# Layer 0's causal mask of natural scores as 32 constant rows of their stacks, and values in frames of 27 columns that fill one output bank

## The reference

```python
scores = jnp.einsum('bhqd,bhkd->bhqk', q, k) / jnp.sqrt(jnp.float32(D))
causal = jnp.tril(jnp.ones((T, T), dtype=bool))
scores = jnp.where(causal, scores, -jnp.inf)
weights = jax.nn.softmax(scores, axis=-1)
out = jnp.einsum('bhqk,bhkd->bhqd', weights, v)
out = out.transpose(0, 2, 1, 3).reshape(B, T, C)
return out @ Wo + bo
```

## Time and profile before

| | |
|---|---|
| median of 3 runs | 495.09 us (494.87 to 496.61) |
| the profiled execution | 494.89 us, of which its span is 493.2 us |
| mean granted TensorE clock | 0.985 |
| TensorE matmul busy | 435.5 us (88%), 3261 instructions |
| VectorE busy | 316.4 us (64%) |
| ScalarE busy | 240.3 us (49%) |
| GpSimd busy | 188.2 us (38%) |
| chain that ended last, by engine | PE 67%, VectorE 12%, DMA 8%, issue 5%, ScalarE 4% |

### The profile page before, as it was taken

The page is one execution under the profiler, slowest core; times in us unless marked ns, Lnnn a source line. Parts: engine busy times, 40 slices in busy tenths (PEclk is TensorE's granted clock), DMA queues, the critical chain, the costliest instruction groups (busy, mean ns, idle before and its releaser), DMA issues.

```text
span 493.2 us, 9895 instructions
## 1 busy us (share of the span) xinstructions
PE 435.5 (88%) x3261; PEld 304.1 (62%) x3261; DVE 316.4 (64%) x955; ACT 240.3 (49%) x565; POOL 188.2 (38%) x234
## 2 busy tenths in 40 slices
PE   1578799997989999999999997999988999999985
PEld 1454446764566576665666655556548999998642
DVE  4555770117577687786877788767565776765753
ACT  2511355444556556554555444445453555555552
POOL 6570120002143543644545451656431444545000
PEclk9999999999899999999999999999998999999987
DMA  5444452325273763623256452142242122211341
GB/s 173 144 97 133 127 134 65 113 77 143 65 183 105 155 180 112 160 85 95 84 158 170 156 152 89 43 128 86 61 122 67 54 77 55 77 50 33 90 131 51
DMA packets 55216, 52.76 MB, mean 107 GB/s; under 512 B 5312, under 2 KB 50000, under 8 KB 55168
## 3 DMA queue, kind: packets, MB, share of 16 engines
q1 hardware_dynamic: 44208, 35.12, 25.7%
q10 hardware_dynamic: 8528, 12.03, 8.6%
q0 software_dynamic: 2432, 5.01, 3.3%
HBM read 33.09 MB, written 19.04 MB: 106 GB/s over the span
## 4 chain that ended last, share of the span: by engine, by line
PE 67%; DVE 12%; DMA 8%; issue 5%; ACT 4%; SPq 2%; POOL 1%; ACTq 0%; DVEq 0%
PE ps_P L1616 8%; PE ps_N L1747 6%; PE ps_N L1549 5%; PE ps_M L1788 3%; DVE NM L1155 3%; PE ps_P L1757 3%; PE ps_M L1757 3%; PE ps_N L1555 3%; PE ps_S L1580 3%; PE ps_N L1560 3%; PE ps_S L1594 3%; PE ps_S L1747 3%; PE ps_M L1659 3%; DMA scm<-MS 2%; PE ps_P L1650 2%
## 5 line engine op out<-in xcount | busy, mean ns | idle before, releaser
L900 ACT ACTIVATE PT<-ps_S 128x512 f32<-128x512 f32 x192 | 112.6, 593 | 114.9 <-PE ps_S L1594 67.2
L1155 DVE TENSOR_REDUCE NM<-ps_N 128x2 f32<-128x512 f32 (+1 forms) x192 | 128.4, 682 | 52.8 <-PE ps_N L1555 34.2
L752 POOL TENSOR_SCALAR_AFFINE_SELECT PT<-PT 128x512 f32<-128x512 f32 x80 | 51.2, 664 | 133.0 <-ACT PT L900 133.0
L1549 PE MATMUL ps_N<-maskb,identb 128*128 128x256 bf16 (+1 forms) x192 | 61.3, 319 | 1.9 <-DVE NM L1155 0.7
L818 POOL DMA_INDIRECT yt<-LATE,EI x39 | 38.5, 988 | 53.9 <-DVE LATE L1383 45.0
L1616 PE MATMUL ps_P<-PT,VA 128*16 128x256 f32 (+1 forms) x1024 | 55.1, 334 | 0.4 <-ACT PT L900 0.4
L1555 PE MATMUL ps_N<-NS 96*128 96x512 f32 x96 | 51.5, 540 | 0.0
L1560 PE MATMUL ps_N<-NS 96*128 96x256 f32 (+1 forms) x128 | 49.5, 427 | 0.0
L1594 PE MATMUL ps_S<-NS 100*128 100x512 f32 (+1 forms) x96 | 46.9, 492 | 0.0
L1616 PEld LDWEIGHTS ps_P<-PT,VA 128*16 128x16 f32 x1024 | 23.5, 96 | 36.1 <-issue 22.4
L1002 ACT ACTIVATE LATE<-ps_N,ucol 128x128 f32<-128x128 f32 x104 | 29.7, 368 | 26.3 <-PE ps_N L1747 26.3
(11 more groups left out here) (191 smaller groups left out, 840.0 us busy)
## 6 DMA issues: line engine op xcount, KB each, us to landing
scr<-XQ SPq DMA_DIRECT2D x24, 256.0 KB
NS<-scr SPq DMA_DIRECT2D x64, 96.0 KB
ROT<-in_L_ffn_W SPq DMA_DIRECT2D x16, 256.0 KB, 3.0
EW<-in_moe ACTq DMA_DIRECT2D x8, 512.0 KB, 3.9
scr<-XQ SPq DMA_DIRECT2D x24, 128.0 KB
NS<-scr SPq DMA_DIRECT2D x8, 384.0 KB
TS<-scr ACTq DMA_DIRECT2D x8, 384.0 KB
TS<-scr ACTq DMA_DIRECT2D x32, 96.0 KB
```

The costliest lines, as they stand in the source:

```text
L752: last = pool.affine_select(out=v, in_=v, compare_op=ALU.is_ge, fill=0.0, base=0, pattern=[[0, 4], [1, P]], channel_multiplier=-1)
L900: act.activation(PT[:, n % NPT, r, :], bank[s][:], ACT.Exp, scale=SCALE).then_inc(exp_ok, 1)
L1155: dve.tensor_reduce(to, x, AX.X, ALU.max, negate=True).then_inc(nm_ok, 1)
L1549: mm(diag, identb[:], maskb[:, None, :].broadcast_to((P, many, P)), start=True, stop=False, skip_group_check=True)
```

## The change

Layer 0's natural scores get the mask through their stacks. The 32 rows behind the 96 of `NS` now hold constants: for the keys a power of two in row `block` of each key, for the queries negative powers of two, so that the product of the 32 rows is a large negative number above the diagonal and cancels elsewhere. The host makes them (`mask_rows`); SyncE loads them (as a new DMA ahead of x's second one), ScalarE rounds them to F32R, SyncE writes them to DRAM and from there, copied 4 and 16 times over, to rows 96 to 127 of both `NS`, all ahead of the first `store`. The mask matmul of layer 0 is gone; where there are two heads by 256 keys, the scores are now two matmuls of 256 columns, the off-diagonal one with 96 rows and the diagonal one with 128. As layer 0 uses the rows now, ScalarE can write the selector rows of `S1` only after layer 0's last natural scores: two of the three at u = 1 of stage 8 and one at u = 1 of stage 9, each just ahead of the copy of the maxima. Layer 1 keeps its mask matmuls.

In `VA` each head has a frame of 27 columns, and `pv` reads 27 columns shifted by 9 for each of the groups 0 to 2, so that the three groups accumulate in the same 27 output partitions of a strip: group g's values stand in rows 9g to 9g + 8. All of the output is in `P0` (groups 0 to 2 in its first 256 columns, group 3 in the others), so there is one `copy_o` at u = 1 and none at u = 10, `otr` has 4 transposes, all into `P1`, and `normalise` has three reciprocals and three products, all behind the fourth transpose. `P1` takes the place of `P0` among the banks of layer 1's experts.

```diff
+VO, VW = 18, 27
+def mask_rows():
+    q, k = (np.zeros((P - QK_ROWS, P), np.float32) for _ in range(2))
+    for i in range(P):
+        block, at = divmod(i, MBLK)
+        k[block, i] = 2.0 ** (32 * at - 48)
+        if at < MBLK - 1:
+            q[block, i] = -2.0 ** (44 - 32 * at)
+        q[block + 1:, i] = -2.0 ** 76
+    return np.stack([np.concatenate([x, x], axis=1) for x in (q, k)], axis=1)
...
-        VA = [sb(f"VA{i}", [P, TPB, NH, 16]) for i in range(NV)]
-        OT = sb("OT", [P, 4 * T])
-        rcp = sb("rcp", [P, TPB, NH])
+        VA = [sb(f"VA{i}", [P, TPB, NH * VW + VW]) for i in range(NV)]
+        OT = sb("OT", [P, 2 * T])
+        rcp = sb("rcp", [P, TPB, 4, 4])
...
             sp.dma_start(K[:, 0:P], table[:, 0:P]).then_inc(id_in, 16)
+            sp.dma_start(LATE[0:P - QK_ROWS, 0:2 * T], rows_d.rearrange("x a t -> x (a t)")).then_inc(raw_in, 16)
             sp.dma_start(X[:, 4:NT, :], x_d[:, 4:NT, :]).then_inc(x_in, 16)
+
+            sp.wait_ge(rows_ok, 1)
+            sp.dma_start(rows_s, MS[1][0:P - QK_ROWS].bitcast(F32)).then_inc(rows_w, 16)
+            sp.wait_ge(rows_w, 16)
+            for i in range(2):
+                to = NS[i][QK_ROWS:P].bitcast(F32)
+                sp.dma_start(to[:, 0:KS, :], rows_s[:, 0:1, :].broadcast_to((P - QK_ROWS, KS, T))).then_inc(rows_in[i], 16)
+                sp.dma_start(to[:, KS:, :], rows_s[:, 1:2, :].broadcast_to((P - QK_ROWS, 16, T))).then_inc(rows_in[i], 16)
...
+            act.wait_ge(raw_in, 16)
+            act.activation(MS[1][0:P - QK_ROWS].rearrange("x a t -> x (a t)"), LATE[0:P - QK_ROWS, 0:2 * T], ACT.Copy).then_inc(rows_ok, 1)
...
                     if k == "lg":
-                        for i in range(1, 5):
+                        ones_rows(1)
+                    if item[:2] == ("mxt", 0) and item[2:] in ((6, 1), (7, 1)):
+                        for i in (2, 4) if item[2] == 6 else (3,):
                             ones_rows(i)
...
             def normalise(L, b):
 
                 n = seq(L, b)
+                await_full(dve, "P1", ("otr", L, b))
+                o = bank["P1"][:].rearrange("p (q e c w) -> p q e c w", q=TPB, e=2, c=4)
+                three = o[:, :, 0, :, 0:27].rearrange("p q c (g d) -> p q c g d", d=HD + 1)
                 for q in range(TPB):
-                    await_full(dve, f"P{q}", ("otr", L, b, q))
-                    o = bank[f"P{q}"][:].rearrange("q (h w) -> q h w", w=32)
-                    link(dve.reciprocal(rcp[:, q, :, None], o[:, :, HD:HD + 1]))
...
+                    dve.reciprocal(rcp[:, q, :, 0:3, None], three[:, q, :, :, HD:HD + 1])
+                link(dve.reciprocal(rcp[:, :, :, 3:4], o[:, :, 1, :, HD:HD + 1]))
...
+                if L == 0:
+                    c, r = heads[0]
+                    ns, at = NS[b % 2], KS + 4 * c + r
+                    if qt > 0:
+                        mm(s[:].rearrange("q (h k) -> q h k", h=many)[:, :, 0:P], ns[0:QK_ROWS, c, q],
+                           ns[0:QK_ROWS, at:at + many, 0:P], start=True, stop=True, skip_group_check=True)
+                    mm(diag, ns[:, c, q], ns[:, at:at + many, w_ - P:w_], start=True, stop=True, skip_group_check=True)\
+                        .then_inc(full[f"N{u % 2}"], 1)
+                    return
...
+                at = 0 if g < 3 else T
...
-                        o = bank[bk][32 * c:32 * c + 16, T * (g % 2) + P * kt:T * (g % 2 + 1)]
+                        w = VW * head + VO - (9 * g if g < 3 else 0)
+                        o = bank["P0"][32 * c:32 * c + VW, at + P * kt:at + T]
...
-                        last = mm(o, va[:, kt, head, :], pr, start=(kt == 0), stop=(kt == 1))
+                        last = mm(o, va[:, kt, w:w + VW], pr, start=(kt == 0 and g in (0, 3)), stop=(kt == 1 and g >= 2),
+                                  skip_group_check=True)
...
                 for q in range(TPB):
-                    await_free(pe, f"P{q}", ("otr", L, b, q))
-                    for g in range(4):
-                        last = pe.transpose(bank[f"P{q}"][:, P * g:P * (g + 1)],
-                                            OT[:, T * g + P * q:T * g + P * (q + 1)], ident)
-                    last.then_inc(full[f"P{q}"], 1)
+                    for j in range(2):
+                        last = pe.transpose(bank["P1"][:, P * (2 * q + j):P * (2 * q + j + 1)],
+                                            OT[:, T * j + P * q:T * j + P * (q + 1)], ident)
+                last.then_inc(full["P1"], 1)
```

More of the change, by code:

```diff
@@ L38 @@
 NV = 3
+VO, VW = 18, 27
 QK_ROWS, ST_ROWS = 96, 104
 KS = 4
+MBLK = 4
 CO_ID, CO_MASK, CO_TRI, CO_ONE = 0, P, 2 * P, 3 * P
@@ L328, with build @@
           "L1_ffn_router_b"]
-def build(nc, w, table, wp_d, moe_d, b2_d, out):
+def build(nc, w, table, wp_d, moe_d, b2_d, rows_d, out):
     ctx = ExitStack()
@@ L463, in build @@
         scr_w = sem("scr_w")
+        rows_in = [sem(f"rows_in{i}") for i in range(2)]
+        raw_in, rows_ok, rows_w = sem("raw_in"), sem("rows_ok"), sem("rows_w")
         ns_in, ts_in = ([sem(f"{n}{i}") for i in range(2)] for n in ("ns_in", "ts_in"))
@@ L923, in again, with copy_o @@
                        .then_inc(ts_in[b % 2], 16)
-            def copy_o(L, b, h):
-                n = seq(L, b)
-                if n >= 1 and h == 0:
-                    await_full(act, "P1", ("otr", *back(L, b, 1), 1))
-                p = f"P{h}"
-                await_full(act, p, ("o", L, b, h))
-                act.activation(OT[:, 512 * h:512 * (h + 1)], bank[p][:], ACT.Copy).then_inc(ocp_ok, 1)
+            def copy_o(L, b):
+                if seq(L, b) >= 1:
+                    await_full(act, "P1", ("otr", *back(L, b, 1)))
+                await_full(act, "P0", ("o", L, b))
+                act.activation(OT[:], bank["P0"][:], ACT.Copy).then_inc(ocp_ok, 1)
             def copy_ont(L, b):
```

72 lines of the change are left out of this document (37 added, 35 removed).

## The result

The changed kernel takes 503.35 us (median of 4 executions, 502.13 to 506.13) beside 495.85 us of the kernel before (4 executions): a ratio of 1.0153, 95% interval 1.0109 to 1.0196. It is slower, by more than the range allowed. The profiled execution took 502.13 us, span 500.1, mean granted clock 0.968 (0.985 before). Two further comparisons gave 1.0117 (1.0057 to 1.0176) and 1.0065 (1.0030 to 1.0101). Ratios leave disturbed executions out, medians don't, which is why the two can differ.

What follows compares the result with a forecast made beforehand. It took layer 0's first half-stages as bound by the maxima's DMA round trip, not TensorE. Terms +0.6 - 2.6 - 2.7 + 1.1 + 1.2 + 1.5 + 0.3 gave -0.6: 494.5 us as a median, range 489.5 to 499.

Steps and rivals of the forecast that it cites:

- the term for ScalarE's selector rows: Selector copies ahead of the maxima's and output's copies: +1.1 us in stage 8, +1.2 in stage 9.
- the rival with the clock: Clock falls in three to five of stages 4 to 9, +3 to +6 us, 497.5 to 500.5; chance 0.20.
- Mask matmuls: Layer 0 units lose 0.22 us (four heads) or 0.11 (two), splitting free: 1.76 us of matmuls a stage.
- The term of `otr`: Four fewer output transposes save 0.44 us in each of 16 attentions, 7.0 in all; none counted in the sum.
- Stages 3 to 7: Layer 0's middle stages each gain 0.54 us on the path: -2.7 us over five.
- The wait for `TS`: TensorE's wait for the maxima's DMA round trip grows from 0.46 to about 1.7 us in stage 5.
- The first rival: The wait for `TS` gives way, first-half savings count too: -3 to -7 us, 488 to 491.5; chance 0.22.
- Start: A 64 KB DMA ahead of x's second part delays the chain by 0.6 us, bounds 0 and 1.5.
- Stage 2, Stage 1: Removed mask matmuls gain 1.3 us in this stage, bounds 0.5 and 1.9.
- Output groups: 27 weight columns add 0.04 us a group (0.77 to 0.81), 1.5 us for the stages from t = 10 on.
- The rival's 5.5 us: All weight loads of 27 columns show, 0.14 us on 56 output groups: +5.5, 500 us; chance 0.05.

Runs made afterwards that it cites:

- e4: Changed kernel with the three selector copies on GpSimd instead of ScalarE, against the kernel before: ratio 0.9963 (0.9919 to 1.0006).
- e14: Changed kernel with the three selector copies on GpSimd, measured again against the kernel before: 501.48 us beside 501.20, ratio 1.0003.
- e7: Changed kernel with 10 and 6 throwaway matmuls in TensorE's waits for the output's copy in stages 8 and 9, against the kernel before: ratio 1.0166.
- e5: The kernel before, unchanged, profiled on a second chip: 494.19 us.
- e13: The changed kernel measured a third time, against the kernel before: 504.97 us beside 501.20, ratio 1.0065.
- e1: Kernel before with only the 27-column frames and one output bank, mask matmuls kept, against the kernel before: ratio 0.9993.
- e17: Changed kernel, selector copies on GpSimd, throwaway matmuls ahead of the waits for `rwB` and `TS`, against the kernel before: 499.57 us beside 501.17, ratio 0.9961.
- e15: Mask rows without frames, selector copies on GpSimd, against the kernel before: 503.18 us beside 501.20, ratio 1.0028.
- e8: Changed kernel, selector copies on GpSimd, maxima's write ahead of the stores, router constants early, against the kernel before: ratio 1.0063.
- e12: Changed kernel, maxima's round trip ahead of the stores, router constants early, copies on GpSimd, constant rows' DMA behind x's second part, against the kernel before: 1.0112.
- e16: Changed kernel, copies on GpSimd, router constants early, second half's maxima through ScalarE's queue, against the kernel before: 503.12 us beside 501.20, ratio 1.0019.
- e3: Kernel before with only its three ScalarE selector copies moved to stages 8 and 9, against the kernel before: ratio 1.0078.
- e9: Changed kernel with only the second half's maxima round trip ahead of the stores in stages 2 to 7, against the kernel before: ratio 1.0218.
- e18: Kernel before with throwaway matmuls ahead of the waits for `rwB` and `TS`, against the kernel before: ratio 1.0025.

## Why the prediction was wrong

The sum said -0.6 us, the first pair of traces has +6.9. Of the 7.5 us between them 3.9 lie at the start and in stages 1 and 2, 2.4 in stages 3 to 7, 3.3 in stages 8 and 9, and 2.1 go the other way behind them. The start's part is not firm (stage 3 begins at 110.3 to 112.5 us in three profiles of the changed kernel, at 110.6 and 110.7 before). The part of stages 8 and 9 is: it is in every profile, and e4 and e14 give most of it back.

**The step that failed** is the term for ScalarE's selector rows, +1.1 us in stage 8 and +1.2 in stage 9 (measured: +3.3 to +3.8 and +1.2 to +1.9), together with the chance of 0.20 for the rival with the clock. The mechanism was named and its bare wait was right: with the clock held up (e7) stage 8 is +1.5, and stage 9 without a fall +1.25. But I summed the wait as if TensorE came out of it at the speed at which it went in. With the fall stage 8 is +3.3 to +3.8. The rival with the clock had a price per fall (+1.0 to 1.4; 1.8 or more in stage 8 by e7's one profile) and had stage 8's idle 2 us in it, yet I counted it as a case beside the sum rather than as a part of this term. It came as it said, with falls in three of the stages 4 to 9 (5, 8 and 9), but at 502 us and not at 497.5 to 500.5. A wait of 2 us with a fall seen behind 2.95 us in the same trace should have gone into the sum with its fall. That a fall follows is a matter of odds: in the three profiles of the changed kernel it did behind stage 8's 2.54 us three times of three, behind stage 9's 1.64 us once of three, and behind the seven waits of 1.0 to 1.9 us for `TS` four times.

**Mask matmuls.** "A unit with four heads loses 0.22 us, one with two heads 0.11", with nothing for the split, was wrong by size. From a unit's first matmul to the next `st` behind it, two-head units took 0.34 us and take 0.32; four-head units 0.46 and 0.34 (medians of stages 4 to 7 in the first pair of traces, without the units in a fall). One two-head unit of the kernel before, from e5's timeline:

```profile
174.15 0.27 PE L1549 MATMUL ps_N<-maskb,identb 128*128 128x256 bf16 x1
174.18 0.48 PE L1555 MATMUL ps_N<-NS 96*128 96x512 f32 x1
174.50 0.40 PE L1580 MATMUL ps_S<-TS 98*128 98x512 f32 x1
```

And one of the changed kernel, from e13's:

```profile
170.79 0.36 PE L1596 MATMUL ps_N<-NS 96*128 96x256 f32 x1
170.99 0.29 PE L1598 MATMUL ps_N<-NS 128*128 128x256 f32 x1
171.11 0.40 PE L1625 MATMUL ps_S<-TS 98*128 98x512 f32 x1
```

From 174.15 to 174.50 and from 170.79 to 171.11. That is 8 x 0.02 + 4 x 0.12 = 0.64 us a stage, not 1.76: a matmul that is taken out and replaced by a split frees little. The term of `otr` was right (0.51 us for 0.93 to the next start). Both together are 1.06 us, which is what stage 6 gained; the sum had 2.2. Matmul busy time fell by 5.8 us (435.5 to 429.7), not by about 19; part of that is that matmuls in a fall take longer.

**Stages 3 to 7**, forecast -2.7, came to nothing: -0.3 in the first pair, and 97.0 us against 97.1 as means. The wait for `TS` was forecast at 1.7 in stage 5 and was 1.44: right there, 1.15 and 1.01 in the other two profiles, and e1 has such waits with its mask matmuls in place. What I had wrong is that it would bind evenly. In stages without it the gain is 1.0 to 1.7 us (stage 4: 20.12 to 18.46; stage 6: 19.26 to 18.28); those with it (1.0 to 1.9 us, in two or three places of each profile of the changed kernel) are between 0.6 us shorter (stage 5 of e13: 18.50) and 0.5 longer (stage 7: 18.46 to 19.00) if no fall follows, and 1.3 or more longer if one does (stage 5: 19.12 to 20.44). The first rival (the wait gives way) and the second (the clock) were both true, in different stages of the same execution, and cancel.

**Start**: x's second part was +1.4, within its bounds but not the +0.6 taken. Stage 2 gained 0.5 us for the 1.3 forecast. Stage 1 is 1.0 longer instead of 1.3 shorter, and one more group of its dispatch matmuls, at 51.75, took 2.47 us where it took 1.31, nearly the ratio of the two levels of the clock. e17, whose kernel is the changed one up to stage 3, has this group at 1.31 us and its stage 1 at 25.82 us for 27.16: these 1.3 us differ between executions of the same code. Of 3.9 us of error 0.8 is the DMA; the rest was not separated by a run.

**Output groups**: forecast 0.81 us a group; from stage 10 to the end the kernel is 0.3 shorter, not 1.5 longer, and e1 and e15 show the frames at nothing. From one group's start to the next instruction's it is 0.776 us before and 0.784 after (medians of 49): 0.008 us and not 0.04, so the wider loads are all but hidden. (The rival's 5.5 us was 0.14 x 56 less 2, which is 5.8.)

By the Trainium skill ("TensorE: Matmul & The Clock Gate", the HAM clock gate) weight loads can go ahead of running matmuls; e1's 0.9993 agrees. Its section on HAM oscillation was read as a fall behind every wait, 500.5 us. The case that it describes has DMA waits of some 3 to 5 us. Here stage 5 agrees (a wait of 1.44 us for `TS`, mean granted clock 0.92), while stage 7, with 1.52 us, kept 1.00; stages 8 and 9 (0.86 and 0.92) fell behind waits for ScalarE.

## What to carry to other kernels

Price a wait that a change opens on TensorE together with the fall of the clock behind it, if the trace shows one fall behind a wait of like length: by the one profile that separates them, the fall cost more than the wait (1.8 us or more against 1.5). Before moving "free" work of another engine to a later place, look at what stands behind it in that engine's order: three copies of 1 us cost 3.5 of the 3.8 us by medians. And count a saved matmul by the distance between the starts of its neighbours, not by its own time, and only as far as the next wait of the stage; if that is a DMA round trip, changing the queue's order only moved it here (e8 to e12, e16). Measure a variant twice before a gain of 0.4% is put down to an edit: e4 and e14 are one kernel, at 0.9963 and 1.0003.

## What the runs showed of the hardware that was not expected

Executions of one kernel spread by 5 to 10 us (498.3 to 504.6 for the kernel before on one chip), and profiles of one kernel differ in which stages hold a clock fall: by the granted clock, three profiles of the changed kernel lost 5.1, 5.1 and 3.4 us of it in stages 3 to 7.

The mean granted clock of an execution says little about its time. Of 35 executions of the kernel before on one chip, nine have a mean under 0.97, with a median time of 501.0 us, and the other 26 have 501.4. One reason is in the traces. The profile's clock reads 1.00 until its first entry, at 48.1 us in the trace before and at 54.9 us in the one after, although the matmuls ahead of it ran at half speed (the same dispatch group takes 2.47 us ahead of it and 1.31 behind). In seven other profiles (e3, e7, e9, e13 to e15, e18) the first entry comes at 22 to 23 us; for some 3 us the matmuls run at full speed (32 of them for the routing take 4.37 us in e13, 7.00 in the first trace after), and then the clock reads 0.50 for 20 us or more. Such an execution has the lower mean, and where both kinds were seen of one kernel it begins its stage 2 earlier (55.2 us in e13 for 57.4 and 56.7, and 53.95 in e14 for 56.55 in e4).

Chips differ as well: on those where the kernel before takes 501 us, stages 12 to 14 take 63.8 to 65.9 us in the profiles of e1, e13 and e18, where they take 59.1 in the first trace, whatever the kernel.

The lowest ratios are those of e17 (0.9961) and e4 (0.9963), the variant with the selector copies on GpSimd with and without fillers; nothing larger was found, and e14's 1.0003 for the latter leaves open whether this is a gain at all.
